# Attention and expert kernel: TensorE issues the first pass's score tile one step ahead, between the second pass and the expert work

## The reference

```python
xn = layernorm(x)
# attention, 16 heads of 16 features, per batch: 32 head units in all
scores = q @ k.T * SCALE + rel * slope          # causal: -inf above the diagonal
attn = maximum(softmax(scores, axis=-1), 1e-10)
s = (attn @ v) @ out_w.T + out_b
# mixture of experts on the same xn: 32 experts, top 4, capacity 128
y[e] = (silu(buf[e] @ w_gate[e]) * (buf[e] @ w_up[e])) @ w_down[e]
out = scatter_add(y * w_topk) + sigmoid(x @ w_sg) * (silu(x @ sw_gate) * (x @ sw_up)) @ sw_down
return x + s * silu(xn + out)
```

## Time and profile before

| | us |
|---|---|
| median of three runs | 668.21 |
| profiled execution: its time | 669.19 |
| profiled execution: span from first to last instruction | 667.6 |
| PE busy, of the span | 575.4 (86%) |
| ACT busy | 456.2 (68%) |
| DVE busy | 463.7 (69%) |
| mean granted TensorE clock | 0.944 of 2.4 GHz |

### The profile page before, as it was taken

The page is one execution under the profiler, slowest core; times in us unless marked ns, Lnnn a source line. Parts: engine busy times, 40 slices in busy tenths (PEclk is TensorE's granted clock), DMA queues, the critical chain, the costliest instruction groups (busy, mean ns, idle before and its releaser), DMA issues.

```text
span 667.6 us, 17966 instructions
## 1 busy us (share of the span) xinstructions
PE 575.4 (86%) x4904; PEld 421.1 (63%) x4904; DVE 463.7 (69%) x1030; ACT 456.2 (68%) x1049; POOL 275.6 (41%) x636
## 2 busy tenths in 40 slices
PE   1698578569999899999999999999999999998981
PEld 1694237236777667776767777677667677766660
DVE  5988955558767776777687768767776876775223
ACT  2321663468888788878888888878888888884320
POOL 7620000043445545544554555454445545553024
PEclk9869879559999999999999999999999999999897
DMA  8990356632443433343344335333433443323178
GB/s 252 162 270 24 117 162 187 176 128 51 98 94 86 100 81 93 84 104 88 85 100 111 84 81 105 85 93 82 107 87 86 105 105 82 82 43 91 17 205 122
DMA packets 78641, 72.00 MB, mean 108 GB/s; under 512 B 18098, under 2 KB 68980, under 8 KB 78580
## 3 DMA queue, kind: packets, MB, share of 16 engines
q1 hardware_dynamic: 68388, 58.81, 32.2%
q0 software_dynamic: 10224, 12.85, 12.9%
HBM read 48.34 MB, written 25.17 MB: 110 GB/s over the span
## 4 chain that ended last, share of the span: by engine, by line
PE 57%; ACT 15%; DVE 9%; issue 8%; DMA 6%; SPq 3%; POOL 1%; ACTq 1%; POOLq 0%; DVEq 0%
PE PSB L812 8%; PE PSB L750 8%; PE PSB L851 7%; ACT PSB L994 7%; PE PSB L724 7%; ACT PB L1003 5%; PE PSB L772 5%; PE PSB L822 4%; PE PSB L746 4%; PE PSB L769 4%; PE PSB L720 3%; PE PSB L843 3%; PE PSB L625 2%; DVE WDS L1194 2%; SPq L481 1%
## 5 line engine op out<-in xcount | busy, mean ns | idle before, releaser
L1259 DVE TENSOR_REDUCE NEGM<-PSB 128x1 f32<-128x1024 f32 (+7 forms) x256 | 191.5, 751 | 71.0 <-PE PSB L724 64.1
L994 ACT ACTIVATE PSB<-PSB,NEGM 128x1024 f32<-128x1024 f32 (+7 forms) x256 | 183.4, 716 | 29.6 <-DVE NEGM L1259 29.6
L1003 ACT ACTIVATE PB<-PSB 128x128 f32<-128x128 f32 (+7 forms) x256 | 167.4, 654 | 52.8 <-PE PSB L750 39.5
L1265 DVE TENSOR_SCALAR PB<-PB 128x128 f32<-128x128 f32 (+7 forms) x256 | 114.9, 459 | 47.6 <-ACT PB L1003 43.1
L724 PE MATMUL PSB<-STACKS 111*128 111x512 bf16 (+3 forms) x384 | 109.9, 343 | 0.0
L750 PE MATMUL PSB<-STACKS 111*128 111x512 bf16 (+3 forms) x384 | 105.2, 328 | 0.0
L746 PE MATMUL PSB<-MK,IDB 128*128 128x128 bf16 x256 | 57.3, 224 | 27.3 <-ACT PSB L994 15.5
L1536 POOL DMA_INDIRECT moe_rows<-YE,IDX x32 | 56.1, 1752 | 46.9 <-issue 46.9
L720 PE MATMUL PSB<-MQ,IDB 128*128 128x128 bf16 x256 | 59.3, 232 | 10.5 <-ACT PSB L994 9.9
L769 PE MATMUL PSB<-PB,VH 128*32 128x256 f32 x640 | 68.2, 384 | 0.0
L746 PEld LDWEIGHTS PSB<-MK,IDB 128*128 128x128 bf16 x256 | 24.8, 97 | 59.5 <-ACT PB L1003 19.5
(11 more groups left out here) (194 smaller groups left out, 1237.8 us busy)
## 6 DMA issues: line engine op xcount, KB each, us to landing
STACKS<-q_parts SPq DMA_DIRECT2D x192, 32.0 KB, 1.8
STACKS<-k_parts SPq DMA_DIRECT2D x192, 32.0 KB, 1.8
WG<-in_L_ffn_w_gate_dram SPq DMA_DIRECT2D x32, 176.0 KB
WU<-in_L_ffn_w_up_dram SPq DMA_DIRECT2D x32, 176.0 KB
WDS<-in_L_ffn_w_down_dram SPq DMA_DIRECT2D x32, 176.0 KB
q_parts<-PB SPq DMA_DIRECT2D x8, 384.0 KB, 2.6
XN<-in_L_attn_qkv_dram SPq DMA_DIRECT2D x4, 512.0 KB, 5.8
moe_rows<-XN SPq DMA_DIRECT2D x1, 2048.0 KB, 8.5
```

Source lines behind the costliest of these rows:

```text
L994: act.activation(sc, sc, ACT.Exp, bias=NEGM[:, par, i:i + 1], accum_out=LSUM[:, par, i:i + 1]).then_inc(exp1_done, 1)
L1003: act.activation(PB[:, k % 2, prob_offset(s):prob_offset(s) + (s + 1) * P], psf[:, base:base + (s + 1) * P], ACT.Exp).then_inc(exp2_done, 1)
L1259: dve.tensor_reduce(NEGM[:, par, i:i + 1], psf[:, base:base + (i + 1) * P], AX_X, ALU.max, negate=True).then_inc(max_ready, 1)
L1265: dve.tensor_scalar(p, p, FLOOR, 0.0, ALU.subtract, ALU.max).then_inc(clamp_done, 1)
```

## The change

In PE's `phase`, step s no longer begins with its own first-pass tile. It issues `pass2(k, s)`, then the first-pass tile of the next step, `pass1(k+2, s+1)`, and then the fillers of step s. The last step of a phase issues step 0 of the following unit, `pass1(k+3, 0)`. The tile of step 0 of unit 2 is issued once ahead of all phases, and one phase instead of two is peeled off ahead of the loop, so that unit k + 3 exists in each of the loop's phases. The waits inside `pass1` and `pass2`, the PSUM banks and the lists of the other four engines stay as they are.

```diff
@@ -881,10 +881,12 @@
             def phase(it, k):
 
                 for s in range(NQ):
-                    if exists(it, k + 2):
-                        pass1(it, k + 2, s)
                     if exists(it, k):
                         pass2(it, k, s, exists(it, k + 2))
+                    if s + 1 < NQ and exists(it, k + 2):
+                        pass1(it, k + 2, s + 1)
+                    if s + 1 == NQ and exists(it, k + 3):
+                        pass1(it, k + 3, 0)
                     if s == 0 and exists(it, k - 1):
                         values(it, k - 1, 0)
                     if s == 1 and exists(it, k - 1):
@@ -902,7 +904,8 @@
                     if s in (6, 7) and exists(it, k):
                         shared(it, k, SB, s - 6)
 
-            phases(pe, phase)
+            pass1(0, 2, 0)
+            phases(pe, phase, 1)
             for g in range(NT // 2):
                 project(g)
```

## The result

The changed kernel takes 722.39 us (median of four, 721.30 to 723.29) against 668.54 us for the kernel before (median of four): a ratio of 1.082, with a 95% interval of 1.076 to 1.089. The forecast was 712 us, with a range of 698 to 726. Lines of the changed kernel carry higher numbers from L883 on: `exp1` is now L997, `exp2` L1006, `weigh` L1054, `row_max` L1262. In the experiments they differ again by a few: L996 to L1001 is always `exp1`, L720 and L721 the bias of `pass1`, L746 and L747 that of `pass2`.

A forecast was written before the change was run, and what follows sets the result against it. PE was taken to bound the steady part, with ACT's list from `weigh` on ending last in three of four phases. 22 x 1.41 + 7 x 1.45 + 1.4 = 42.6 us on 669.19 gave 711.8, stated as 712 us, range 698 to 726.

The forecast's parts named there:

- the fourth: Phases with k % 4 = 3, where PE has longer fillers and no idle time: forecast +1.45 us each.
- Step 1: `expert_down` moves back behind the first-pass tile of step 2, making `weigh` start 0.38 us later in phases 1 to 29.
- W: The start of `weigh` on ACT in a phase, from which the prediction counts times.
- Step 2: Tile of step 3, now ahead of the fillers, waits for `exp1` of step 1: new 1.45 us PE stall each phase.
- W': The start of `weigh` in the changed kernel, forecast 0.38 us later than W.
- Steps 3 and 4: From the stall to `pass2` step 4: 1.03 us later from W in ordinary phases, 1.07 where k % 4 = 3.
- Steps 4 to 7: Tile waits late in the phase and the later `c_transpose`: taken as 0, upper bound 0.1 us a phase.
- Phase 0: No `weigh` there, but the same wait of step 3's tile for `exp1` of step 1: 1.4 us, between 0 and 3.
- the rival: PE's clock falls in each phase because of the new gaps: 41 us on top, 753 us; chance 0.06.
- Only W moving: Stall at step 3 covered, only 0.38 us reaching `pass2` step 4 in 22 ordinary phases: 8 us, 677; chance 0.06.
- the faster rival: Early maxima let ACT finish `exp1` of step 3 sooner, removing waits at `pass2` step 4: 651 us; chance 0.04.

The follow-up runs named there:

- down_first: The changed kernel with `expert_down` issued ahead of the first-pass tile of step 2: 710.91 us, ratio 1.070 to the kernel before.
- all_but_3: The changed kernel with the first-pass tile of step 3 back at its old place: 687.20 us, ratio 1.034 to the kernel before.
- only_3: The kernel before with only the first-pass tile of step 3 moved one step ahead: 701.70 us, ratio 1.058.
- all_but_6: The changed kernel with the first-pass tile of step 6 back at its old place: 712.77 us, ratio 1.072 to the kernel before.
- gather_16: The changed kernel with the expert-row gather fetching 16 rows instead of 128 from unit 2 on: 715.31 us, ratio 1.076 to the kernel before.
- values_spread: The kernel before, old tile order, half of values batch 0 moved to step 1 and batch 1 to step 3: 676.63 us, ratio 1.016.

## Why the prediction was right, and where its sum was short

*What bounds the kernel.* Right for the stretch up to `pass2` step 4. The chain from `expert_down` over `weigh` to `exp1` of step 3 decides in the ordinary phases, PE's own work in the fourth; moving `expert_down` alone moves the time (down_first). Behind step 4 the shift rows bound the changed kernel, which the prediction did not have.

*Step 1, W later.* Forecast 0.38 us, measured 0.28 and 0.44 in the two phases of the table and 0.40 in the mean of phases 1 to 29; down_first takes back 11.2 us of this stretch.

*Step 2, the new stall.* Forecast at W' + 1.69, found at W + 1.61 in both phases; forecast 1.45 us each, measured 1.47 in every fourth phase, 1.32 in the others and 1.21 in phase 1, 39.2 us over 29 waits. all_but_3 and only_3 show that it is this tile.

*Steps 3 and 4.* Forecast `pass2` step 4 at W' + 5.47 and W' + 6.13, found at W + 5.42 and W + 6.15. ACT's extra idle time ahead of `exp2` of step 3, forecast as 1.1 us, is 0.82.

*Steps 4 to 7.* This is the term that was mis-sized. I took 0 with 0.1 us a phase as the bound; it is 0.6 to 0.8 us in ordinary phases and 0.32 in the fourth, 15.9 us in all. In the fourth phases it is mostly the wait of the tile of step 6 for `exp1` of step 4 (all_but_6 takes back 0.26 of the 0.32). In phase 10 that wait is small: the tile is issued at 324.96 and could have gone 0.39 us (the length of this step before) behind 324.44, so 0.13 us. The larger part there is the sentence that the later `c_transpose` is "hidden as long as the shifts land before the next phase": they don't. Two things come together. `c_transpose` stands 3.11 us behind `pass2` step 4 instead of 2.79, since the tile of step 6 and its wait are now ahead of it; putting this tile back (all_but_6) saves 9.2 us of the third stretch. And the shift rows land later, because the gather is now issued with them; almost removing it (gather_16) saves 7.5.

I had no row for the landing of the shift rows, which should have been a bound and not a zero. The kernel before had no margin there. In phase 10 `pass2` step 0 was issued at 311.39. PE's tile ahead of it ran to 310.71 + 0.60 = 311.31 and `exp2` of step 7 to 311.15, and 311.39 is 3.91 us behind `c_transpose`; with the gather cut, PE gets the shift rows 3.8 to 3.9 us behind it. So they must have come just about when PE did, and any delay had to show. What I missed in the mechanism: a stall of PE does not shift the phase as a whole. It shifts PE against POOL, whose gather keeps near W, and so brings two transfers together that were 1.64 us apart.

*Phase 0.* Forecast 1.4 us, for the same wait of the tile of step 3. That wait was not there: PE's only wait at L720 in this phase is 0.3 us, at the tile of step 2. The phase took 14.03 us for 13.44 but began 0.61 us earlier, so phase 1 starts at 157.84 for 157.86: nothing.

*The sum.* 42.6 us forecast, 53.8 measured between the spans. 15.9 short for steps 4 to 7; 1.0 over for W and the way to step 4 (40.2 us for 41.2); 1.4 over for phase 0; and 2.4 that the two executions differ outside. What was gained (DVE's and ACT's waits) was valued at 0, and that held. One slip stands in the last step: 711.8 lies 1 us above the median by the prediction's own words, which gives 711 and not 712.

*The rivals.* The clock stayed at 1.00 in the steady part with gaps of 1.2 to 1.5 us in phases 1 to 29, so neither the rival nor the Trainium skill's warning (TensorE: Matmul & The Clock Gate, "A second HAM failure mode: psum-queue depth-cycling") came true here. Only W moving would have been the first stretch alone, 11.6 us, and the stall at step 3 was not covered. For the faster rival the wait of `pass2` step 4 did carry a gain, but not by earlier tiles: it took other fillers.

## What to carry to other kernels

An instruction issued early on an in-order engine brings its wait with it, and all that stands behind it pays; before moving it, look up when the thing it waits for ends, not only when its own result is wanted. A waiting consumer (64.1 us on DVE, 41.4 on ACT) is worth nothing unless its list is the one that ends last. And when one engine's list slips against another's, look at which transfers now meet: a landing time that no row shows must be bounded from both sides, since what hid it may have hidden it by very little (here by some 0.1 us in ordinary phases).

## What was unexpected of the hardware

PE could go on 3.8 to 3.9 us behind `c_transpose` (DVE copy, 2.07 us for SP to issue three copies of 2 KB to STACKS, landing) with the gather cut to 16 rows, and mostly 4.1 to 4.3 us behind it with a 128-row indirect gather issued within 0.25 us of the first copy. When the gather came 1.4 to 1.6 us behind the first copy (all_but_3), it was again mostly 3.8 to 3.9 us. The longest were not those issued together: with the gather 0.7 to 0.9 us behind the first copy (values_spread) it was mostly 4.6 to 4.8 us.
